# A two-layer graph and feed-forward kernel: the second graph's edge columns packed without rounding each tile to chunks

## The chip, the cores and the metric

The kernel runs on one core of a Trainium2 chip. The metric is device time in microseconds (us) of one execution; the median of three is given, and one further execution was profiled. A core has TensorE (PE in the profile; PEld are its weight loads), VectorE (DVE), ScalarE (ACT), GpSimd (POOL) and SyncE (SP). SP computes nothing: here it starts DMAs and passes on semaphores.

## The reference

Four layers work in turn on x (6250 nodes by 256), each one adding its result to x; each takes the layer norm of x.

```python
# first graph: attention over incoming edges, with encoded edge attributes
alpha = (h_src . a_src) + (h_dst . a_dst) + sum(relu(edge_attr @ edge_W.T + edge_b) * h_dst)
# feed-forward 1: 64 slice tokens for each of 8 heads, attention among the tokens, back to the nodes
# second graph: 106250 edges, 8 heads, no edge attributes
s_u = x @ W_u.T + b_u
s_v = x @ W_v.T
e = leaky_relu(s_u[src] + s_v[dst], 0.2)
probs = exp(e - segment_max(e, dst)[dst]) / segment_sum(exp(...), dst)[dst]
out = segment_sum(x[src] * probs, dst)
# feed-forward 2: 8 experts, the best two for each node
```

Both graphs have the same edges, sorted by their destination. A node's degree is its number of incoming edges, 17 on average.

## The kernel before

**Nodes in tiles.** `sort_nodes` sorts the nodes by degree and puts them into 49 tiles of 128 nodes, one node to a partition. A tile has as many edge columns as its largest degree; column j of a partition holds the j-th edge of its node, or a stand-in for none (source N, a row of zeros whose score is a very low number). For the inputs of the reference the largest degrees of the 49 tiles, counted from `dst`, run from 9 to 35: 9, 10, 11, three of 12, three of 13, four of 14, four of 15, five of 16, five of 17, five of 18, four of 19, three of 20, three of 21, two of 22, two of 23, 25, 26 and 35. They sum to 851.

**Columns in chunks.** C = 4 columns are a chunk. Each tile is rounded up to whole chunks, at least three: 232 chunks or 928 columns in all. `windows` writes them to the array `slots` in DRAM, 64 bytes (4 records of 4 words) for a partition and chunk. `K["ct"]` and `K["lt"]` hold the first and the last chunk of each tile.

**A graph stage** (`graph`, called for layer 0 and layer 1) works through the chunks in order, with R = 4 buffers:

- SP (`load`, L863) brings a chunk's records into `recs`, and (`relay`, L868) passes on that a chunk's rows have landed.
- POOL (`gather`, L900) starts four indirect DMAs per chunk, one for each column; each fetches for 128 partitions the row of the source node. Before it refills a buffer it waits for `msg_ok` of the chunk four places earlier.
- DVE (`body`) makes the scores (L1170, L1172), the running maximum over the tile's chunks (L1176), the differences (L1177); ACT takes the exponentials (L1055); DVE multiplies the rows by them (`messages`, L1133) and rescales the sums that are in PSUM (`rescale`, L1139).
- PE (`aggregate`, L945) adds the chunk's messages to those sums with the identity as weights: four matmuls of 264 columns in fp32, shown as eight.

`by_tile` runs these bodies: the first chunk of a tile (it opens it), a hardware loop (`Fori`) over those between, the last one (it closes it). In the body that opens a tile, DVE also finishes the tile before (`finish`, L1143 to L1157 and L135), after ACT has copied its sums out of PSUM (L1022).

**Between the graphs** stands `slice_ffn`. It is a row of blocks, each with one program for an engine, and at a block's end all engines wait for one another. The block at L1286 (the tokens' sums) has programs for PE, ACT and DVE; SP has none in it and waits at its end. The next blocks, L1447 and L1551, work on the tokens and write the rows of the second graph.

A loop of SP that the prediction uses stands in `windows`, L767 to L773: for each tile one `value_load` of a number into a register, one DMA to an address computed from it, then a wait until that DMA has landed.

Of the kernel before, what the change touches and what calls it, by code (L numbers as in the profile page):

```python
# [11 lines left out]
F32 = mybir.dt.float32  # L12
# [8 lines left out]
E = 106250  # L21
# [27 lines left out]
LEAST = -(-2 * N // Q) // 2 * 2  # L49
KC = HID // 128  # L50
# [30 lines left out]
def take(eng, sem):  # L81

    eng.wait_ge(sem, 1)
    eng.sem_inc(sem, -1)  # L84
# [78 lines left out]
def sort_nodes(nc, K, ins, dr):  # L163


    with ExitStack() as stack:
# [58 lines left out]
        deep = m.sb("o_deep", [1, QT])  # L225
        aim = m.sb("o_aim", [1, QT])
        reach = m.sb("o_reach", [1, QT])
# [30 lines left out]
        with nc.Block() as block:  # L258
# [83 lines left out]
            def _(dve):  # L342
# [90 lines left out]
                ch.link(v.reduce_max(dmax[:], pD[0:QT, :], axis=AX))  # L433
                ch.link(v.tensor_scalar(ci[:], dmax[:], float(C - 1), None, ALU.add))
# [18 lines left out]
                ch.link(v.tensor_scalar(reach[:], pC[:, 2, 0:QT], -3.0, None, ALU.add))  # L453
                v.scalar_tensor_tensor(K["pl"][:], pC[:, 0, 0:QT], 8.0, reach[:], ALU.mult, ALU.add)
                ch.link(v.tensor_scalar(deep[:], pC[:, 2, 0:QT], float(WIN - 1), None, ALU.is_ge))
                ch.link(v.scalar_tensor_tensor(aim[:], pC[:, 0, 0:QT], 3.0, spare[:], ALU.add, ALU.subtract))
                ch.link(v.tensor_tensor(aim[:], aim[:], deep[:], ALU.mult))
                v.tensor_tensor(K["dc"][:], aim[:], spare[:], ALU.add)
# [126 lines left out]

FIRST = 33
# [8 lines left out]
def windows(nc, K, ins, dr, m, dall, ew, recT, ew_in, own_in):  # L595
# [33 lines left out]
    pB = m.ps("x_pB", [Q, 512])  # L629
    w_in = T("w_in"); bxb_ok = T("bxb_ok"); w_ok = T("w_ok"); wch = T("wch")  # L630
# [32 lines left out]
    with nc.Block() as block:  # L663
# [19 lines left out]
        def _(pe):  # L683
            t_ = nc.tensor
            pe.wait_ge(bxb_ok, 1)
# [8 lines left out]
        def _(dve):  # L694
# [4 lines left out]
            v.memset(ew[:], 0.0).then_inc(ew_zero, 1)  # L699
            v.memset(recT[:], 1.0)  # L700
# [3 lines left out]
            wx.link(v.reciprocal(temp, temp))  # L704
            dve.wait_ge(w_ok, 1)
# [77 lines left out]
def graph(nc, K, ins, dr, layer):  # L783
# [7 lines left out]
    with ExitStack() as stack:  # L791
# [27 lines left out]
        else:  # L819
            sdst, norm, wr, raw = K["sdst"], K["norm1"], K["wr"], K["raw"]  # L820
            fin = m.sb(L + "fin", [Q, D])
            turned = m.sb(L + "turned", [128, 2, Q])
# [10 lines left out]
        row_of = lambda ap: ap.rearrange("p a h -> p (a h)")  # L833

# [22 lines left out]
        with nc.Block() as block:  # L857
            @block.sync
            def _(sp):
                n2 = groups(sp, K)  # L860

                def load(u, r):
                    sp.dma_start(recs[:, r, :], dr["slots"][:, bass.ds(4 * u + r, 1), :].rearrange("q a c -> q (a c)").bitcast(F32)).then_inc(rec_in[r], 16)  # L863
# [25 lines left out]
            def _(pool):  # L889
                n2 = groups(pool, K)  # L890
# [22 lines left out]
            def _(pe):  # L913
                t_ = nc.tensor
                n2 = groups(pe, K)
# [21 lines left out]
                def aggregate(i, b):  # L937

                    pe.wait_ge(msg_ok, i + 1)
                    pe.sem_inc(pace, 1)  # L940
# [32 lines left out]
                def body(t, i, opens, closes, ends):  # L973
# [3 lines left out]
                    aggregate(i, bass.ds(i % 2, 1))  # L977
# [125 lines left out]
            def _(dve):  # L1103
# [3 lines left out]
                dve.wait_ge(w_zero, 2)  # L1107
                heads = lambda ap: ap.rearrange("p (c h) -> p c h", h=H)
# [16 lines left out]
                def messages(i):  # L1125

                    b2, b4 = bass.ds(i % 2, 1), bass.ds(i % R, 1)
# [32 lines left out]
                def body(t, i, opens, closes, ends):  # L1160
# [18 lines left out]
                    if first_layer:  # L1179
# [6 lines left out]
                        messages(i)  # L1186
# [4 lines left out]
                    messages(i)  # L1191
# [1012 lines left out]
```

## Time and profile before

| what | us |
|---|---|
| median of 3 executions | 4076.98 (4074.56 to 4084.47) |
| the profiled execution, its own time | 4077.23 |
| its span, first to last instruction | 4075.5 |
| gathers of the second graph, first and last start | 1998.7 and 3159.7 |
| SP's wait at the end of the block at L1286 | 219.6 |

The span is the stretch that the profile's records cover; the execution's own time is 1.7 us more. Stages can be told apart by the tile names: `g_rows<-own` are gathers of the first graph, `g_rows<-rows` those of the second, `f_` the first feed-forward, `e_` the experts.

### The profile page before, as it was taken

Reading aid. Unit: us, or ns where it says so; the run is one execution under the profiler, and the core shown is the slowest. Engines: PE = TensorE matmul, PEld = TensorE weight load, DVE = VectorE, ACT = ScalarE, POOL = GpSimd, SP = SyncE. Lnnn points to the kernel's source line nnn. Section 1 sums busy time; section 2 is a strip of 40 time slices with the busy share of each in tenths; the row PEclk is TensorE's granted clock in tenths of the full one; section 3 lists DMA queues with packets and bytes.
Section 4 is the critical chain, followed back from the end, with each engine's and each line's share of the span. In section 5 each row is a group of like instructions: output and inputs, shape, how many; then the busy total and the mean of one; then the engine's idle time right before and its main releaser. Section 6 shows DMA issues by size and latency. Waiting matters only on the chain. (4 is left out here: it accounts for less than half of the span.)

```text
span 4075.5 us, 69197 instructions
## 1 busy us (share of the span) xinstructions
PE 2987.4 (73%) x12787; PEld 2165.0 (53%) x12788; DVE 2290.8 (56%) x5023; ACT 1295.0 (32%) x5485; POOL 2294.7 (56%) x2343
## 2 busy tenths in 40 slices
PE   4624777788888877989666656566665489999998
PEld 3422444444444444658544444444444388888887
DVE  4534888888888887864355555555555611111111
ACT  1402444444444444432211111111111533333333
POOL 5156777677777772002577777777777523333332
PEclk9857999899999998988777877877777799999999
DMA  8545444344444442000244444444444766665564
GB/s 185 152 92 131 114 115 113 100 106 105 105 105 105 108 108 53 0 2 32 78 112 113 113 113 113 113 112 113 113 113 112 216 186 168 166 170 165 170 174 123
DMA packets 284454, 477.32 MB, mean 117 GB/s; under 512 B 143854, under 2 KB 185660, under 8 KB 283892
## 3 DMA queue, kind: packets, MB, share of 16 engines
q0 software_dynamic: 127312, 321.61, 32.2%
q1 hardware_dynamic: 148203, 151.72, 12.7%
q10 hardware_dynamic: 8880, 3.34, 0.4%
q8 instruction: 21, 0.34, 0.0%
q14 instruction: 38, 0.31, 0.0%
HBM read 426.29 MB, written 50.68 MB: 117 GB/s over the span
## 5 line engine op out<-in xcount | busy, mean ns | idle before, releaser
L945 PE MATMUL g_pA<-g_msg,k_ident 128*128 128x264 f32 (+1 forms) x3712 | 1153.1, 464 | 475.5 <-DVE g_pA L1139 411.6
L945 PEld LDWEIGHTS g_pA<-g_msg,k_ident 128*128 128x128 f32 x3712 | 808.4, 229 | 808.7 <-issue 661.9
L900 POOL DMA_INDIRECT g_rows<-own,g_recs x928 | 879.4, 948 | 333.9 <-issue 262.8
L900 POOL DMA_INDIRECT g_rows<-rows,g_recs x928 | 879.6, 948 | 296.6 <-issue 194.7
L934 PE MATMUL g_pE<-g_ew,g_recT 128*128 128x512 f32 x932 | 515.4, 680 | 242.1 <-DVEq L1123 238.8
L1133 DVE TENSOR_TENSOR g_msg<-g_rows,g_pp 128x1024 f32 (+3 forms) x464 | 571.9, 1233 | 151.4 <-DVEq L84 151.3
L1983 POOL DMA_INDIRECT out<-e_ys,e_goal x102 | 160.6, 1575 | 505.8 <-issue 486.3
L934 PEld LDWEIGHTS g_pE<-g_ew,g_recT 128*128 128x128 f32 x932 | 171.4, 203 | 459.1 <-DVEq L1123 331.2
L2036 PE MATMUL e_pY<-e_w,e_hT 128*128 x1632 | 373.8, 382 | 35.5 <-issue 35.5
L1055 ACT ACTIVATE g_pp<-g_dd 128x32 f32<-128x32 f32 x464 | 95.2, 205 | 918.5 <-ACTq L84 918.5
L2025 PEld LDWEIGHTS e_pH<-e_xT,e_w 128*128 128x128 f32 x3264 | 381.6, 192 | 5.2
L2025 PE MATMUL e_pH<-e_xT,e_w 128*128 128x128 f32 x3264 | 381.9, 275 | 0.0
L2122 DVE TENSOR_TENSOR e_ys<-e_pY,k_x 128x256 f32<-128x256 f32 x102 | 43.3, 425 | 581.8 <-PE e_pY L2036 575.4
L2036 PEld LDWEIGHTS e_pY<-e_w,e_hT 128*128 128x128 f32 x1632 | 302.0, 190 | 84.1 <-issue 47.1
L1166 DVE TENSOR_REDUCE g_al<-g_prod 128x32 f32<-128x1088 f32 x232 | 297.1, 1280 | 57.7 <-DVEq L84 57.7
L1118 DVE SCALAR_TENSOR_TENSOR g_prod<-g_pE,g_dall 128x1024 f32<-128x1024 f32 x232 | 284.2, 1225 | 20.6 <-DVEq L84 7.8
L1069 ACT ACTIVATE g_pA<-g_pA,g_cs 128x33 f32<-128x33 f32 x1464 | 276.3, 277 | 4.4
L1006 ACT ACTIVATE g_recT<-g_pRT 16x128 f32<-16x128 f32 x234 | 62.2, 266 | 541.4 <-ACTq L84 541.0
L2078 ACT ACTIVATE e_hT<-e_pH,e_b 128x128 f32<-128x128 f32 x816 | 221.7, 382 | 39.3 <-issue 36.5
L2065 ACT ACTIVATE e_xT<-e_pX,e_bl,e_gl 128x128 f32<-128x128 f32 x204 | 82.2, 453 | 462.0 <-PE e_pX L2008 462.0
L1170 DVE TENSOR_TENSOR g_al<-g_rows,k_sdst 128x32 f32 (+1 forms) x232 | 45.0, 194 | 287.0 <-DVEq L84 282.3
L1561 POOL MEMSET f_bu<- 128x16 f32 x1 | 0.1, 111 | 288.7 <-POOLq L113 288.7
(419 smaller groups left out, 3533.5 us busy)
## 6 DMA issues: line engine op xcount, KB each, us to landing
e_w<-in_L_ffn_W SPq DMA_DIRECT2D x110, 1024.0 KB
g_rows<-own,g_recs POOLq DMA_INDIRECT x928
g_rows<-rows,g_recs POOLq DMA_INDIRECT x928
g_recs<-slots SPq DMA_DIRECT2D x468, 8.0 KB
tok<-e_xall SPq DMA_DIRECT2D x7, 910.0 KB
own<-p_row SPq DMA_DIRECT2D x50, 119.0 KB
p_x<-in_x SPq DMA_DIRECT2D x1, 5600.0 KB
own<-p_x SPq DMA_DIRECT2D x1, 5600.0 KB
```

What stands on the lines that cost most here:

```text
L900: pool.indirect_dma_start(out=rows[:, r, j, :], out_offset=None, in_=rows_d, in_offset=bass.IndirectOffsetOnAxis(ap=recs[:, r, 4 * j:4 * j ...
L934: last = t_.matmul(pE[:, c:c + 512], recT[:], ew[:].rearrange("p c d -> p (c d)")[:, c:c + 512], start=True, stop=True)
L945: last = t_.matmul(sums, K["ident"][:], of, start=False, stop=(j == C - 1), skip_group_check=True)
L1055: s.activation(pp[:, 0:C * H], dd[:, 0:C * H], ACT.Exp).then_inc(pp_ok, 1)
L1069: last = s.activation(of[:, h, :], of[:, h, :], ACT.Copy, scale=cs[:, h:h + 1])
L1118: v.scalar_tensor_tensor(to, pE[:].rearrange("p (c h w) -> p c h w", c=C, h=H), 0.0, over(by_head(own), 1, C), ALU.max, ALU.mult).then_inc ...
L1133: v.tensor_tensor(to, of, by, ALU.mult).then_inc(msg_ok, 1)
L1166: ch.link(v.reduce_sum(sc, prod[:], axis=AX))
L1983: pool.indirect_dma_start(out=out, out_offset=bass.IndirectOffsetOnAxis(ap=goal_b[b][:, 0:1], axis=0), in_=ys[:, b, :], in_offset=None, bo ...
L2025: last = t_.matmul(pH[b][c][:, j, :], w1[:, b, k, units], xT[:, b, k, :], start=(k == 0), stop=(k == 1))
L2036: last = t_.matmul(pY[b][:], hT[:, b, k, :], w2[:, bass.ds(e, 1), k, :].rearrange("p a h -> p (a h)"), start=(k == 0), stop=(k == KC - 1))
L2078: last = s.activation(hT[:, b, c * HK + j, :], pH[b][c][:, j, :], ACT.Gelu, bias=b1[:, bass.ds(e, 1), c * HK + j])
```

## The change

The second graph no longer reads `slots` but a new array `cols`, in which the tiles' columns follow one another with no rounding. A tile has max(largest degree, 8) columns, so there are 851, in 213 chunks; gathers go by groups of four chunks, so 54 groups or 216 chunks are fetched. `K["at"]` holds the first column of each tile, `K["ends_in"]` the chunk in which the tile before it ends. A chunk in which one tile ends and the next begins is fetched once and worked on twice: by the body that closes the one (columns past its end are masked with `past`) and by the body that opens the other (columns ahead of its start are masked with `ahead`). This is done at all 48 borders, also where a tile ends with a chunk; there are 213 + 48 = 261 bodies in place of 232. The buffer of a shared chunk comes free with the second of them, and POOL now waits for the semaphore `freed`, which PE raises in `aggregate`.

`cols` is filled by a new program for SP in the block at L1286 of the kernel before: for each tile it copies the tile's chunks from `slots` to `cols`, DRAM to DRAM, to the tile's first column, and waits until all of them have landed, since the next tile's copy overwrites what the last chunk has beyond its columns.

Smaller edits: `sort_nodes` and `windows` compute the new tables; `past` and `ahead` are made by five DVE instructions at the second graph's start; the memset of `oz` stands later in its block; some buffers share memory.

```diff
@@ windows: DVE
+            dve.wait_ge(pF_ok, 1)
+            v.tensor_copy(K["at"][:], pF[:, 0:QT + 1])
+            wx.link(v.tensor_scalar(K["ends_in"][:], pF[:, 0:QT + 1], -1.0, None, ALU.add))
+            wx.link(v.tensor_scalar(K["ends_in"][:], K["ends_in"][:], CLOG, None, ALU.arith_shift_right))
@@ graph
+        at = (lambda t, i: i) if first_layer else (lambda t, i: i + t)
         def bounds(eng, t):
+            if not first_layer:
+                last_of = lambda x: eng.value_load(K["ends_in"][0:1, bass.ds(x, 1)], min_val=1, max_val=COLS // C)
+                return 0 if isinstance(t, int) and t == 0 else last_of(t), last_of(t + 1)
@@ graph: POOL
-                            pool.wait_ge(msg_ok, 4 * (u - 1) + (r + 1))
+                            pool.wait_ge(done, 4 * (u - 1) + (r + 1))
@@ graph: PE
                     pe.wait_ge(msg_ok, i + 1)
-                    pe.sem_inc(pace, 1)
+                    pe.sem_inc(freed if frees else pace, 1)
...
-                    aggregate(i, bass.ds(i % 2, 1))
+                    aggregate(i + t, bass.ds((i + t) % 2, 1), not closes)
@@ graph: DVE, before the first body
+                    mc.link(v.scalar_tensor_tensor(inside[:], K["ends_in"][:], -float(C), K["at"][:], ALU.mult, ALU.add))
+                    mc.link(v.tensor_tensor(past[:], over(K["iota64"][:, 0:C], 1, QT), over(inside[:, 1:QT + 1], 2, C), ALU.is_ge))
...
@@ graph: DVE, body
-                        take(dve, rows_ok)
+                        if start or not opens:
+                            take(dve, rows_ok)
...
+                    if not first_layer and (closes or opens and not start):
+                        of = (past if closes else ahead)[:, bass.ds(t, 1), :]
+                        ch.link(v.tensor_tensor(heads(sc), heads(sc), over(row_of(of), 2, H), ALU.add))
@@ slice_ffn: a program for SP in the block of the tokens' sums
+                    def piece(chunk, col, n, put):
+                        sp.dma_start(dr["cols"][:, bass.ds(col, C * n), :].rearrange("q a c -> q (a c)"),
+                                     dr["slots"][:, bass.ds(chunk, n), :].rearrange("q a c -> q (a c)")).then_inc(put, 16)
+                    with sp.Fori(0, QT) as t:
+                        chunk = sp.value_load(K["ct"][0:1, bass.ds(t, 1)], min_val=0, max_val=CMAX - 2 * WIN)
+                        close = sp.value_load(K["lt"][0:1, bass.ds(t, 1)], min_val=2, max_val=CMAX - WIN)
+                        col = sp.value_load(K["at"][0:1, bass.ds(t, 1)], min_val=0, max_val=COLS)
+                        with sp.Fori(chunk, close + 1) as i:
+                            piece(i, nc.s_assert_within(col + C * i - C * chunk, 0, COLS), 1, packed)
+                        sp.wait_ge(packed, 16 * close + 16)
+                        sp.sem_inc(pace, 1)
```

What stood in SP's row between the loads of the first feed-forward's weights (L1250) and the load of the next block (L1450), before:

```order
L1250 DMA f_wqkv<-in_L0_ffn_W_q 64x64
L1250 DMA f_wqkv<-in_L0_ffn_W_k 64x64
L1250 DMA f_wqkv<-in_L0_ffn_W_v 64x64
L1243 UNCONDITIONAL_BRANCH
L1448 UNCONDITIONAL_BRANCH
L1450 DMA f_bout<-in_L0_ffn_b_out 128x256
```

And of the change, in the same place, from the third of three such loads of a table into a register (`k_ct` and `k_lt` are loaded just above it) to the end of the loop over tiles (L1334); the loop over a tile's chunks is L1338:

```order
L1337 TENSOR_LOAD k_at
L1337 ISA x2
L1338 UNCONDITIONAL_BRANCH
L1338 ISA
L1339 REGISTER_ALU
L1339 ISA
L1332 ISA
L1332 DMA cols<-slots 128x16
L1338 ISA
L1338 COMPARE_AND_BRANCH
L1340 ISA
L1334 REGISTER_ALU
```

SP has gained a loop with a wait inside (L1340 sets up the wait for the landing), run 49 times, in a block in which it did nothing.

On DVE, the body that closes a tile of the second graph, before:

```order
L1170 ISA
L1170 TENSOR_TENSOR g1_al<-g1_rows,k_sdst 128x32
L1172 SCALAR_TENSOR_TENSOR g1_al<-g1_al 128x32
L1176 TENSOR_REDUCE g1_mx<-g1_al 128x8
L1177 TENSOR_TENSOR g1_dd<-g1_al,g1_mx 128x40
L1133 ISA
L1133 TENSOR_TENSOR g1_msg<-g1_rows,g1_pp 128x1056
L1139 TENSOR_TENSOR g1_pA<-g1_pA,g1_cs 128x8x33
```

And of the change:

```order
L1207 ISA
L1207 TENSOR_TENSOR g1_al<-g1_rows,k_sdst 128x32
L1211 TENSOR_TENSOR g1_al<-g1_al,g1_past 128x32
L1212 SCALAR_TENSOR_TENSOR g1_al<-g1_al 128x32
L1216 TENSOR_REDUCE g1_mx<-g1_al 128x8
L1217 TENSOR_TENSOR g1_dd<-g1_al,g1_mx 128x40
L1169 ISA
L1169 TENSOR_TENSOR g1_msg<-g1_rows,g1_pp 128x1056
L1175 TENSOR_TENSOR g1_pA<-g1_pA,g1_cs 128x8x33
```

One small instruction has come in (L1211); the body that opens a tile has gained its like with `g1_ahead`. The bodies between are as they were.

## Rows read from the trace of the kernel before

**Rows 1.** The page: span, and busy time by engine (share of the span)

```profile
span 4075.5 us, 69197 instructions
PE 2987.4 (73%) x12787; PEld 2165.0 (53%) x12788; DVE 2290.8 (56%) x5023; ACT 1295.0 (32%) x5485; POOL 2294.7 (56%) x2343
```

**Rows 2.** Windows: the tokens' block, then the second graph

```profile
core 0: us, PE busy (x) PEld busy (x) DVE busy (x) ACT busy (x) POOL busy (x), PEclk, DMA share, GB/s
1590.00:1809.00 219.00, 211.06 (x882) 139.09 (x882) 175.84 (x298) 93.75 (x197) 0.00 (x0) 0.98 0.00 1
1998.00:3164.00 1166.00, 703.57 (x2125) 506.34 (x2126) 621.63 (x1577) 161.60 (x885) 879.59 (x928) 0.78 0.45 113
```

**Rows 3.** Line L900 in the second graph: durations ns, first and last start

```profile
L900 POOL DMA_INDIRECT g_rows<-rows,g_recs x928: 942/946/1189, 1998.7 to 3159.7; - x186
  issue: 194.7, 639
```

**Rows 4.** Timeline of DVE: a closing body, an opening one, a middle one

```profile
2512.97 0.19 DVE L1170 TENSOR_TENSOR g_al<-g_rows,k_sdst 128x32 f32 x1 [3.40 <-DVEq L84]
2513.19 0.19 DVE L1172 SCALAR_TENSOR_TENSOR g_al<-g_al 128x32 f32<-128x32 f32 x1
...
2517.03 0.19 DVE L1170 TENSOR_TENSOR g_al<-g_rows,k_sdst 128x32 f32 x1 [0.91 <-DVEq L84]
...
2518.56 1.25 DVE L1133 TENSOR_TENSOR g_msg<-g_rows,g_pp 128x1056 f32 x1 [0.64 <-DVEq L84]
2521.02 0.17 DVE L1143 TENSOR_SCALAR g_den<-g_accf 128x8 f32<-128x8 f32 x1 [1.20 <-DVEq L84]
...
2523.38 0.20 DVE L1170 TENSOR_TENSOR g_al<-g_rows,k_sdst 128x32 f32 x1
...
2526.48 0.19 DVE L1170 TENSOR_TENSOR g_al<-g_rows,k_sdst 128x32 f32 x1
```

**Rows 5.** Timeline of PE in the same stretch

```profile
2516.47 3.88 PE L945 MATMUL g_pA<-g_msg,k_ident 128*128 x8 [4.29 <-DVE g_pA L1139]
...
2526.88 2.04 PE L945 MATMUL g_pA<-g_msg,k_ident 128*128 x8 [1.59 <-DVE g_pA L1139]
```

**Rows 6.** Timeline of all engines: middle bodies that follow at once

```profile
3098.39 0.18 DVE L1170 TENSOR_TENSOR g_al<-g_rows,k_sdst 128x32 f32 x1
...
3098.82 3.56 PE L945 MATMUL g_pA<-g_msg,k_ident 128*128 x8 [3.53 <-DVE g_pA L1139]
...
3102.78 0.44 DVE L1139 TENSOR_TENSOR g_pA<-g_pA,g_cs 128x264 f32<-128x264 f32 x1 [1.59 <-DVEq L84]
...
3103.53 0.19 DVE L1170 TENSOR_TENSOR g_al<-g_rows,k_sdst 128x32 f32 x1 [0.30 <-DVEq L84]
```

**Rows 7.** Timeline of DVE: last middle body of tile 5, its closing body

```profile
2087.31 0.19 DVE L1170 TENSOR_TENSOR g_al<-g_rows,k_sdst 128x32 f32 x1
...
2090.95 0.19 DVE L1170 TENSOR_TENSOR g_al<-g_rows,k_sdst 128x32 f32 x1 [0.49 <-DVEq L84]
```

**Rows 8.** Timeline: a chunk's fourth gather, and its scores

```profile
2528.36 0.95 POOL L900 DMA_INDIRECT g_rows<-rows,g_recs  x1 [0.30 <-issue]
...
2531.48 0.19 DVE L1170 TENSOR_TENSOR g_al<-g_rows,k_sdst 128x32 f32 x1 [1.71 <-DVEq L84]
```

**Rows 9.** Waits of SP: total us, times, longest

```profile
SPq L1286 <- PEq L1286: 219.6, 1, 219.6
```

**Rows 10.** Timeline of SP: start, then first issue to end of last

```profile
100.28 25.89 SPq L280 DMA_DIRECT2D own<-p_row  x38
...
317.54 9.94 SPq L771 DMA_DIRECT2D slots<-x_win  x3
```

**Rows 11.** Line L771, SP's loop with a wait: last its landing times

```profile
L771 SPq DMA_DIRECT2D slots<-x_win x3: 342/343/348, 317.5 to 327.1; - x3
...
DMA to landing us min/median/max: 3.0/3.3/3.4
```

**Rows 12.** Line L770, the register load of that loop

```profile
L770 SPq FUSED_REGOPS  x6: 37/102/164, 316.6 to 326.6; - x6
L770 SPq TENSOR_LOAD <-k_dc x3: 273/275/275, 316.7 to 326.3; - x3
L770 SPq SEQ_ASSERT  x3: 18/18/18, 317.2 to 326.8; - x3
```

**Rows 13.** DMA issues: KB each, median us to landing

```profile
slots<-x_more SPq DMA_DIRECT2D x1, 64.0 KB, 1.6
```

More of the change, by code:

```diff
@@ L684, in _ @@
             t_ = nc.tensor
+            pe.wait_ge(wide_ok, 1)
+            t_.matmul(pF[:, 0:QT + 1], colw[:], K["tri"][0:QT, 0:QT + 1], start=True, stop=True).then_inc(pF_ok, 1)
             pe.wait_ge(bxb_ok, 1)
@@ L821, in graph @@
             fin = m.sb(L + "fin", [Q, D])
+            inside = m.sb(L + "inside", [Q, QT + 1])
+            past = m.sb(L + "past", [Q, QT, C])
+            ahead = m.sb(L + "ahead", [Q, QT, C])
+            masks = m.sem(L + "masks")
             turned = m.sb(L + "turned", [128, 2, Q])
@@ L859, in _ @@
             def _(sp):
-                n2 = groups(sp, K)
+                n2 = groups(sp, K) if first_layer else column_groups(nc, sp, K)
                 def load(u, r):
-                    sp.dma_start(recs[:, r, :], dr["slots"][:, bass.ds(4 * u + r, 1), :].rearrange("q a c -> q (a c)").bitcast(F32)).then_inc(rec_in[r], 16)
+                    of = dr["slots"][:, bass.ds(4 * u + r, 1), :] if first_layer else dr["cols"][:, bass.ds(4 * C * u + C * r, C), :]
+                    sp.dma_start(recs[:, r, :], of.rearrange("q a c -> q (a c)").bitcast(F32)).then_inc(rec_in[r], 16)
                 def relay(u, r):
@@ L889, in _ @@
             def _(pool):
-                n2 = groups(pool, K)
+                n2 = groups(pool, K) if first_layer else column_groups(nc, pool, K)
+                done = msg_ok if first_layer else freed
                 def gather(u, first):
@@ L914, in _ @@
                 t_ = nc.tensor
-                n2 = groups(pe, K)
+                n2 = groups(pe, K) if first_layer else None
                 def transpose(u, r):
@@ L1107, in _ @@
                 dve.wait_ge(w_zero, 2)
+                if not first_layer:
+                    mc = Chain(dve, masks)
+                    mc.link(v.scalar_tensor_tensor(inside[:], K["ends_in"][:], -float(C), K["at"][:], ALU.mult, ALU.add))
+                    mc.link(v.tensor_tensor(past[:], over(K["iota64"][:, 0:C], 1, QT), over(inside[:, 1:QT + 1], 2, C), ALU.is_ge))
+                    mc.link(v.tensor_tensor(ahead[:], over(K["iota64"][:, 0:C], 1, QT), over(inside[:, 0:QT], 2, C), ALU.is_lt))
+                    mc.link(v.tensor_scalar(past[:], past[:], -LOW, None, ALU.mult))
+                    mc.link(v.tensor_scalar(ahead[:], ahead[:], -LOW, None, ALU.mult))
                 heads = lambda ap: ap.rearrange("p (c h) -> p c h", h=H)
@@ L1185, in body @@
                         take(dve, pp_ok)
-                        messages(i)
+                        messages(t, i)
                         if not ends:
@@ L1190, in body @@
                     take(dve, pp_ok)
-                    messages(i)
+                    messages(t, i)
                     if opens:
@@ L1285, in slice_ffn, with _ @@
             g3 = lambda ap: ap.rearrange("p (h g) -> p h g", h=FH)
+            packed = T("packed"); last_packed = T("last_packed")
             with nc.Block() as block:
+                @block.sync
+                def _(sp):
+                    def piece(chunk, col, n, put):
[9 more added lines that the diff above has]
+                        sp.sem_inc(pace, 1)
+                    piece(sp.value_load(K["end"][:], min_val=0, max_val=CMAX - WIN), sp.value_load(K["at"][0:1, QT:QT + 1], min_val=0, max_val=COLS), 4, last_packed)
+                    sp.wait_ge(last_packed, 16)
                 @block.tensor
@@ L1520, in _ @@
                     v.tensor_tensor(g3(at[:]), g3(pq[:]), over(red[:], 2, G), ALU.subtract).then_inc(exp_in, 1)
+                    v.memset(oz, 0.0)
                     dve.wait_ge(exp_out, 1)
@@ L1698, in experts @@
             hot = [m2.sb(f"e0_hot{k}", [Q, QT, X]) for k in range(2)]
-            both = m2.sb("e0_both", [Q, QT, X])
+            both = K["sdst"]
             best = [m2.sb(f"e0_best{k}", [Q, QT]) for k in range(2)]
@@ L2162, in program @@
               "slots": scratch("slots", (Q, CMAX + 3 * QT, REC), I32),
+              "cols": scratch("cols", (Q, COLS + 16 * C, C), I32),
               "tok": scratch("tok", (1 + NPAD, XW))}
```

47 lines of the change are left out of this document (28 added, 19 removed).

## The prediction

> **What bounds the kernel now.** I read the page first, for the span [rows 1]. No engine is busy throughout, so the stages must be told apart. Two matter here, and the windows show them [rows 2]. In the block of the tokens' sums PE is busy for 211 of 219 us, and the DMA share is 0.00: PE bounds it, and SP and the DMA engines do nothing. In the second graph no engine reaches 80% busy, yet POOL is the bound. That takes the line's own view: 928 gathers start between 1998.7 and 3159.7, one each 1161/927 = 1.252 us, of which 0.946 us is the instruction and 0.3 us is put down to issue (194.7 us in 639 times) [rows 3]. The reader is to see that POOL never stands still: a chunk of four gathers takes 5.0 us, 232 chunks take 1161 us, and that is the stage.
>
> Next, how near the others are. The timeline of DVE gives the time from one body to the next where nothing holds it up. From the body that closes a tile to the first middle body of the next it is 2523.38 - 2512.97 = 10.4 us, with the opening body between; from a middle body to the next it is 3.10 us [rows 4]. The first of these was with PE at 1.2 GHz (eight matmuls in 3.88 us); at 2.4 GHz they take 2.04 us [rows 5]. Where PE is at 1.2 GHz a middle body takes 5.14 us, since the rescaling must wait for the sums of the body before [rows 6]. From the last middle body to the closing one I read 3.64 us [rows 7]. The granted clock over the stage is 0.78 of full speed [rows 2], so both kinds occur.
>
> **The second graph after the change.** POOL starts 864 gathers in place of 928: 64 x 1.252 = 80 us less. It gets this only if the bodies keep up, and there are 29 more of them. A tile with k bodies costs DVE: closing to first middle 10.4 us, less at most 1.2 us with PE at 2.4 GHz (the opening body's messages end at 2519.81, so `finish` cannot start much sooner than that, where it started at 2521.02 [rows 4]), plus two masks. A mask is one instruction of 128x32 like L1172, at 0.19 us and a gap: 0.22 us. I take 10.3 us. Last middle to closing costs 3.7 us, and each further middle body lies between 3.10 and 5.14 us; I take 3.5 us, nearer the lower end, because PE has less idle time when bodies follow at once. So a tile costs 14.0 + 3.5 (k - 3) us, against 1.252 us of POOL for each column.
>
> The first 22 tiles (largest degree 9 to 16) have 301 columns and, counting the borders, 97 bodies. DVE needs 22 x 14.0 + 31 x 3.5 = 416.5 us, POOL 377 us: DVE falls 40 us behind. From there the two go about level (a tile of 17 columns and 5 bodies: 21.0 against 21.3 us), and only the last tiles give time back. The four buffers take up part of the lag: a chunk's scores can start 3.1 us after its fourth gather [rows 8], that is 6.9 us after its first; its buffer is wanted 20 us after its first, 13 us later, and a body holds it for 3 us: about 10 us. POOL is then held up by some 32 us, and the stage gets 80 - 32 = 48 us shorter. The bounds: with every body at 2.4 GHz (13.3 + 3.1 (k - 3)) the lag is about 12 us, nearly all taken up, and the gain is 78 us. With middle bodies at 4.0 us the lag reaches some 80 us by the same sum and the gain is about 10 us; with all at 5.1 us the stage would be longer than now, which I leave out of the range, since PE would then hardly be idle and its clock would rise.
>
> The hand-over of a buffer through PE (`freed`) costs POOL nothing where PE waits for the messages anyway. What DVE does before its first body, the five mask instructions of at most 128x196, lies beside the first gathers, which have to land first.
>
> **The copy.** Here the change adds a chain of its own, in a block that is 219.6 us long for SP [rows 9]. SP waited there for the others; now it has 49 tiles with 232 DMAs, and the others will wait for it.
>
> Per DMA: 38 DMAs with one computed address were issued in 25.89 us, 0.68 us each, some waiting included [rows 10]. The new one has a second address and sits in a loop with a branch at each turn; I add 0.27 us (four short register instructions with their gaps, of the kind of 37 to 102 ns each [rows 12]): 0.95 us, 232 x 0.95 = 220 us. Bounds 0.85 and 1.05 us.
>
> Per tile: three register loads. One is 0.275 + 0.16 + 0.02 us with gaps [rows 12], 0.65 us with its address; three are 1.95 us. Then the wait for landing. The nearest loop in the trace, one load, one DMA, one wait, takes (9.94 - 0.34)/2 = 4.8 us a turn [rows 10], of which 3.3 us is landing [rows 11]. That leaves 1.5 us for load, address and branch, which bears out these prices. How long a 64-byte piece takes from DRAM to DRAM no row shows. The rows around it are 1.6 us for the 64 KB of `x_more` [rows 13] and 3.3 us for the 24 KB pieces of `x_win`, which were issued beside POOL's gathers. In the new place nothing else uses the DMA engines, so I take 2.0 us, of which 0.7 us lies under the DMA's own issue and the inner branch: 1.3 us. Control of both loops and the semaphores: 0.85 us. Together 4.1 us, 49 x 4.1 = 201 us. With the last piece of four chunks and its wait (4 us) the copy takes 220 + 201 + 4 = 425 us and starts with the block. It sticks out of it by 425 - 219.6 = 205 us. Nothing hides that: the next block's first work waits at the barrier. Bounds: 0.85 us and 1.6 us to landing give 197 + 181 + 4 = 382 us, 162 us over; 1.05 us and 3.3 us give 244 + 265 + 4 = 513 us, 293 us over.
>
> The Trainium skill, in "DMA: Bandwidth & Descriptors", gives a fixed cost of about 2.0 us for a DMA (Anatomy of one DMA), and lists 512 B as the least transfer without a read-modify-write (Specifications). The first would leave my sum as it is. The second speaks for a later landing of 64-byte pieces; it is a rival below, priced from rows.
>
> **The rest.** The memset of `oz` moves from the head of its block to a place beside ACT's exponentials; both are under 1 us, and I count nothing. The tables in `sort_nodes` and `windows` are four or five instructions of under 0.3 us beside gathers.
>
> **Sum.** Against the profiled execution's 4077.2 us, which stands level with the median of 4077.0: + 205 - 48 = + 157, so 4234 us.
>
> **Rivals.**
> 1. *Late landing.* Pieces smaller than those of `x_win` land no sooner than these did, 3.3 us, though no gathers run. Then each tile waits 1.3 us longer: 64 us, 4298 us. For it: of the two rows, the one with the smaller pieces has the longer time. Against it: those ran beside other traffic.
> 2. *The bodies eat the gain.* PE stays at 1.2 GHz for most of the stage, middle bodies take 4 us and more, and the second graph saves 10 us or nothing: 4272 to 4282 us. For it: a clock of 0.78 now. Against it: PE's idle time before L945 shrinks when bodies follow at once.
> 3. *The copy is hidden*, and the kernel is faster. SP would have to be through in 219.6 + 48 = 268 us to break even, 5.5 us a tile with its 4.7 DMAs. Were the DMAs 0.5 us each and three loads and the wait 2.9 us, it would be 262 us, and the time 4071; fully hidden it would be 4029. Against it: the loop of L771 needs 4.8 us a turn for one load and one DMA [rows 10, 11]. It decides as soon as a chunk costs less than 0.5 us in all.
> 4. *The packing does nothing for the gathers*: POOL is still held up at each border, and only the copy is left. This is rival 2 at its end.
>
> **How the numbers follow.** The forecast, copy 380 to 460 us and a gain of 20 to 78 us, has 60%: its own range is 4165 to 4290. Rival 1 has 20%, rival 2 12%, rival 3 6%; 2% for anything else. 80% lie between 4170 and 4310: the lower end is the quick copy with nearly the full gain, the upper the late landing and little gain. 0.3% is 12 us, about what can be told from no change. Faster by more than that only in rival 3: 6%. Within it 1%. Slower 93%.
>
> **What would show it.** In the block of the tokens' sums the engines' busy time stays as in [rows 2], but the block is some 425 us long, and PE waits for SP at its end. The DMAs from `slots` to `cols` stand 0.9 to 1.0 us apart within a tile and 4 to 5 us across one. The gathers are 864, and between first and last start some 1113 us; if they take 1082, DVE never held POOL up. The mean time of L945's matmuls tells rival 2 from the forecast. I am wrong if SP's loop is through before PE is, or if the landing is not waited for once a tile.

## The result, and the profile after

The changed kernel takes 4444.73 us (median of 4 runs, 4435.65 to 4456.38) against 4075.77 us before (again the median of 4): ratio 1.0903, 95% interval 1.0871 to 1.0936. It is slower, as predicted, but by 369 us and not by 157; the forecast of 4234 us and its range up to 4310 both miss. The profiled execution took 4440.49 us. From here "before" is the kernel before and "after" the changed one.

The page of after, its first two lines (they answer to [rows 1]):

```profile
span 4438.7 us, 73650 instructions
PE 2993.2 (67%) x13021; PEld 2166.9 (49%) x13022; DVE 2373.9 (53%) x5304; ACT 1305.0 (29%) x5572; POOL 2236.6 (50%) x2279
```

No engine has more to do than before by more than DVE's 83 us, while the span grew by 363: the loss is waiting. Two windows, the tokens' block and the second graph, say where (they answer to [rows 2]):

```profile
core 0: us, PE busy (x) PEld busy (x) DVE busy (x) ACT busy (x) POOL busy (x), PEclk, DMA share, GB/s
1576.00:2168.00 592.00, 211.33 (x882) 139.51 (x882) 175.90 (x299) 93.91 (x197) 0.00 (x0) 0.68 0.04 4
2354.00:3545.00 1191.00, 732.69 (x2382) 518.84 (x2382) 707.23 (x1861) 174.39 (x981) 819.52 (x864) 0.80 0.40 102
```

In the first, PE is busy for the same 211 us as in [rows 2], but the block lasts 592 us in place of 219. In the second, POOL has 64 gathers and 60 us of work less, and the stage is longer all the same. The gathers' own line, first in the first graph, then in the second with what POOL waited for (to [rows 3]):

```profile
L929 POOL DMA_INDIRECT g_rows<-own,g_recs x928: 940/946/1181, 342.9 to 1550.6; - x186
...
L929 POOL DMA_INDIRECT g_rows<-rows,g_recs x864: 940/946/1192, 2355.0 to 3539.2; - x173
its engine sat idle before it (us, times) until:
  issue: 249.2, 762
  PEq L969: 113.3, 91
```

The same line of before, in its first graph:

```profile
L900 POOL DMA_INDIRECT g_rows<-own,g_recs x928: 940/946/1181, 344.3 to 1564.0; - x186
```

These starts cut both spans into stages, of which the last is what follows the last gather (to 4438.7 and 4075.5):

| stage | before, us | after, us | difference |
|---|---|---|---|
| up to the first gather | 344.3 | 342.9 | -1.4 |
| first graph | 1219.7 | 1207.7 | -12.0 |
| between the graphs, with the copy | 434.7 | 804.4 | +369.7 |
| second graph | 1161.0 | 1184.2 | +23.2 |
| behind the last gather | 915.8 | 899.5 | -16.3 |

I had +205 for the third row, -48 for the fourth and nothing for the others.

**The copy.** The line of the DMA (durations in ns, first and last start), and the register operations of the inner loop's own line, two in a turn:

```profile
L1332 SPq DMA_DIRECT2D cols<-slots x233: 547/564/687, 1579.2 to 2165.7; - x117
DMA to landing us min/median/max: 2.0/2.1/3.4
...
L1338 SPq FUSED_REGOPS  x464: 42/156/273, 1578.5 to 2162.7; - x155
```

The waits (us in all, times, longest): SP's for the landing at a tile's end, and PE's behind its own part of the block, before its first matmul of the next.

```profile
SPq L1341 <- DMA cols<-slots: 58.6, 49, 2.2
...
PE f_pA L1516 <- DVE f_sums L1562: 375.9, 1, 375.9
```

SP is at work from 1576 to 2168 us without a pause but for 58.6 us. Its timeline, two DMAs of one tile:

```profile
1597.53 2.40 SPq L1332 DMA_DIRECT2D cols<-slots  x2
```

From the start of the first to the end of the second it is 2.40 us; less one DMA of 0.57, they stand 1.83 us apart. Over all neighbours within a tile the mean is 1.79 us, where I had 0.95.

**The second graph.** DVE's timeline, which answers to [rows 4]. L1207 is the first instruction of a body. The rows are those of one tile from its first middle body on (three middle ones from 2702.02, the closing one at 2712.05), the opening and the first middle body of the next, and then two middle bodies of a later tile; the other instructions and bodies are left out:

```profile
2702.02 0.19 DVE L1207 TENSOR_TENSOR g_al<-g_rows,k_sdst 128x32 f32 x1 [0.20 <-issue]
...
2705.24 0.18 DVE L1207 TENSOR_TENSOR g_al<-g_rows,k_sdst 128x32 f32 x1
...
2708.83 0.19 DVE L1207 TENSOR_TENSOR g_al<-g_rows,k_sdst 128x32 f32 x1 [0.29 <-issue]
...
2712.05 0.18 DVE L1207 TENSOR_TENSOR g_al<-g_rows,k_sdst 128x32 f32 x1
...
2717.01 0.19 DVE L1207 TENSOR_TENSOR g_al<-g_rows,k_sdst 128x32 f32 x1 [1.35 <-issue]
...
2722.86 0.19 DVE L1207 TENSOR_TENSOR g_al<-g_rows,k_sdst 128x32 f32 x1 [0.20 <-issue]
...
2748.82 0.18 DVE L1207 TENSOR_TENSOR g_al<-g_rows,k_sdst 128x32 f32 x1
...
2754.24 0.19 DVE L1207 TENSOR_TENSOR g_al<-g_rows,k_sdst 128x32 f32 x1 [0.40 <-DVEq L86]
```

and PE's in the same stretches (to [rows 5, 6]):

```profile
2705.68 2.04 PE L974 MATMUL g_pA<-g_msg,k_ident 128*128 x8 [1.81 <-DVE g_pA L1175]
...
2712.52 2.04 PE L974 MATMUL g_pA<-g_msg,k_ident 128*128 x8 [1.59 <-DVE g_pA L1175]
...
2749.26 3.88 PE L974 MATMUL g_pA<-g_msg,k_ident 128*128 x8 [2.57 <-DVE g_pA L1175]
...
2754.18 3.88 PE L974 MATMUL g_pA<-g_msg,k_ident 128*128 x8 [1.04 <-DVE g_pA L1175]
```

From a middle body to the next there are three prices. The first pair of a tile takes 3.22 us (2702.02 to 2705.24), since the rescaling finds the opening body's sums ready. A later pair takes 3.59 us with PE at 2.4 GHz (2705.24 to 2708.83; the matmuls between them last 2.04 us), and 5.42 us with PE at 1.2 GHz (2748.82 to 2754.24; 3.88 us), since the rescaling waits for the sums of the body before. Closing to opening is 4.96 us here, opening to middle 5.85. Taking the starts of this line one after another over tiles 0 to 38, where DVE from tile 1 on lags behind the gathers by 7 to 21 us and so nothing but the bodies sets the pace, gives the means below.

| from one body to the next, tiles 0 to 38 | times | predicted, us | after, us | more in all, us |
|---|---|---|---|---|
| closing to opening to middle | 38 | 10.3 | 5.09 + 5.73 | 20 |
| last middle to closing | 39 | 3.7 | 3.82 | 5 |
| middle to middle | 74 | 3.5 | 4.09 (32 of them over 4) | 44 |

In tiles 0 to 38 the 74 pairs of middle bodies fall apart by those prices: 37 are the first of their tile (3.21 to 3.22 us), 5 are later ones at 3.59 us, and 32 are later ones of 4.29 to 5.43 us, 5.18 on the mean, with PE at 1.2 GHz for at least part of the matmuls that are waited for. The 69 us are nearly all of the 71 by which this stage missed its term. The gathers' starts show the same from POOL's side: summed over the chunks, they are 105 us later than one chunk each 5.0 us, where I had 32, and nearly all of it before 3240 us.

### The profile page after: what moved, and what is told of

It reads as the page before. It is cut to its first block and busy times, and to the rows that moved or that the text cites. A ratio compares the mean times of both kernels' runs of the same rounds, so it can differ in the third digit from the quotient of the medians.

```text
span 4438.7 us, 73650 instructions
## 1 busy us (share of the span) xinstructions
PE 2993.2 (67%) x13021; PEld 2166.9 (49%) x13022; DVE 2373.9 (53%) x5304; ACT 1305.0 (29%) x5572; POOL 2236.6 (50%) x2279
## 5 line engine op out<-in xcount | busy, mean ns | idle before, releaser
L974 PE MATMUL g_pA<-g_msg,k_ident 128*128 (+1 forms) x3944 | 1173.5, 449 | 464.2 <-DVE g_pA L1175 336.0
L974 PEld LDWEIGHTS g_pA<-g_msg,k_ident 128*128 128x128 f32 x3944 | 822.8, 219 | 811.4 <-issue 672.4
L929 POOL DMA_INDIRECT g_rows<-rows,g_recs x864 | 819.5, 949 | 378.9 <-issue 249.2
L1169 DVE TENSOR_TENSOR g_msg<-g_rows,g_pp 128x1056 f32 (+3 forms) x493 | 608.2, 1234 | 209.4 <-DVEq L86 209.4
```

The costliest lines, as they stand in the source:

```text
L929: pool.indirect_dma_start(out=rows[:, r, j, :], out_offset=None, in_=rows_d, in_offset=bass.IndirectOffsetOnAxis(ap=recs[:, r, 4 * j:4 * j ...
L974: last = t_.matmul(sums, K["ident"][:], of, start=False, stop=(j == C - 1), skip_group_check=True)
L1169: v.tensor_tensor(to, of, by, ALU.mult).then_inc(msg_ok, 1)
```

## Experiments

All are compared with runs of before on the same chip as theirs (medians 4078.2, 4083.0, 4079.7 and 4080.1 us in the four sets).

**1. The copy alone.** All of the copy, none of the packed reading:

```diff
-n2 = groups(pool, K) if first_layer else column_groups(nc, pool, K)
+n2 = groups(pool, K)
...
-of = dr["slots"][...] if first_layer else dr["cols"][...]
+of = dr["slots"][:, bass.ds(4 * u + r, 1), :]
...
-if not first_layer and (closes or opens and not start):
+if False:
```

> The columns are copied as in the change, but the second graph then reads the slots as before: 232 bodies, no masks, no packed columns (the copied columns are not used). Theory A (the copy block costs what the trace of the changed kernel shows: 592 us where the block took 219.6): 4075.8 + 372 = 4448, less up to 13 us by which the first graph came out shorter there, so 4435 to 4450. Theory B (the copy costs the 205 us of my prediction and the rest of the loss lies in the second graph): about 4281.

Measured: 4421.27 us, ratio 1.0840 (1.0822 to 1.0858). Theory B is out: the copy by itself loses 343 us. The time lies 14 us under A's interval, of which some 9 are that the rest of the change gives back 22 us (experiment 9) and not 13.

**2. Packed reading, and columns that cost nothing.** Eight straight copies in the place of the loop. They leave the columns where they were, so this kernel sums other edges, as many as before, in the 261 bodies of the change (the expectation below has 265 by mistake):

```diff
-with sp.Fori(0, QT) as t:
-    ...
+for k in range(8):
+    sp.dma_start(dr["cols"][:, 108 * k:108 * (k + 1), :]..., dr["slots"][:, 27 * k:27 * (k + 1), :]...)
```

> The second graph is the changed one (packed columns, 265 bodies, masks), but the columns come from 8 straight copies of 27 chunks each and no loop over tiles: arranging the columns is left out, so the sums of the second graph are of other edges, as many as before. Theory A (216 gathered chunks in 265 bodies are no faster than 232, since bodies and not GpSimd bound the first 39 tiles: 1184 us of gathers against 1161): 4075.8 + 23, less up to 13 us of the first graph, so 4080 to 4105. Theory B (the second graph by itself gains the 48 us that I predicted and its loss is an effect of the copy ahead of it): 4015 to 4030.

Measured: 4071.44 us, ratio 0.9978 (0.9949 to 1.0008), ten runs between 4028 and 4087. The second graph took 1187.5 us from first to last gather, as in after (A), and the copy's 370 us are gone. The median lies 9 us under A's interval. The 22 us of experiment 9 in place of 13 would make up for that; by before's 4078.2, the second graph's 26.5 and these 22 it should still be 4083, so 12 us are not explained. The eight DMAs, with fixed addresses and 1728 B a partition, take 0.597 us of SP each:

```profile
L1332 SPq DMA_DIRECT2D cols<-slots x8: 592/597/604, 1577.0 to 1581.5; - x8
```

**3. No wait at a tile's end.** Each chunk goes to its own place, and one wait stands behind both loops. This too leaves out the arranging of the columns:

```diff
-piece(i, nc.s_assert_within(col + C * i - C * chunk, 0, COLS), 1, packed)
-sp.wait_ge(packed, 16 * close + 16)
+piece(i, nc.s_assert_within(C * i, 0, COLS), 1, packed)
...
+sp.wait_ge(packed, 16 * last + 16)
```

> Every chunk is copied to its own place (4 columns a chunk), so that no copy overlaps another and the wait for the landing at each tile's end goes; one wait stands behind the loop. Arranging the columns is left out. Theory A (SP's turns of 1.79 us for each of 232 copies are the cost, and the 49 landing waits, 58.6 us, come on top): 4445 - 56 = 4389, 4378 to 4395; the SP loop takes 535 us instead of 592. Theory B (the transfers themselves are what SP waits for, and its issue slows down because the queue is full): no change, 4440 to 4450. Theory C (the wait also holds the pace of the loop, so that without it the turns get as short as the 0.95 us that I predicted): 4190 to 4210.

Measured: 4316.28 us (four runs, 4300 to 4335), ratio 1.0600 (1.0572 to 1.0628): 128 us less than after, and none of the three theories' numbers. The line of its DMA, and the inner loop's register operations:

```profile
L1332 SPq DMA_DIRECT2D cols<-slots x233: 522/543/682, 1583.0 to 2033.2; - x117
DMA to landing us min/median/max: 1.9/2.0/3.3
...
L1338 SPq FUSED_REGOPS  x464: 42/59/87, 1582.6 to 2030.4; - x155
```

and two DMAs of one tile in its timeline:

```profile
1707.66 1.99 SPq L1332 DMA_DIRECT2D cols<-slots  x2
```

The DMAs now stand 1.99 - 0.53 = 1.46 us apart (1.48 as the mean), since with the wait I also took out the arithmetic on the column (`col + C * i - C * chunk`). Of the two operations of L1338 in a turn one takes 0.04 us in both kernels; the other takes 0.26 us in after and 0.07 here, and an addition on L1339 is gone as well. 0.31 us less for 232 DMAs is 71 us, and the 58.6 us of waits make 130. So nobody waits for the queue (B is out), and the turns come nowhere near 0.95 us (C is out): SP's own instructions are the cost. Beside the DMA's 0.54 to 0.57 us the loop takes 0.93 us a turn here and 1.22 in after.

**4. Matmuls that keep TensorE busy.**

```diff
 last.then_inc(agg_ok, 1)
+if not first_layer:
+    for _ in range(4):
+        t_.matmul(pX[:, 0:128], K["ident"][:], K["ident"][:], start=True, stop=True)
```

> The changed kernel with four matmuls of 128 columns behind the four of each body of the second graph, into a PSUM bank that nothing reads, in the time in which TensorE waits for VectorE's rescaling. Theory A (middle bodies take 4.9 to 5.4 us instead of 3.2 to 3.6 because TensorE runs at 1.2 GHz in them, and a busier TensorE is granted 2.4 GHz more of the time): the second graph comes near GpSimd's bound of 216 x 5.0 = 1082 us, so 30 to 90 us less than the changed kernel: 4355 to 4415, with a granted clock near 1 in the second graph. Theory B (the granted clock does not follow TensorE's work here): the clock stays near 0.80 and the time at 4445 or, where the added 0.9 to 1.8 us a body lie on the chain, up to 4600.

Measured: 4376.80 us, ratio 1.0735 (1.0717 to 1.0753): 68 us less than after, by work that nobody needs. The window of its second graph (the last but two of the numbers is the clock):

```profile
2351.00:3481.00 1130.00, 859.57 (x4470) 728.94 (x4470) 702.48 (x1860) 178.07 (x981) 819.72 (x864) 0.93 0.42 108
```

The granted clock rose from 0.80 to 0.93, POOL's wait for buffers (`PEq L970`) fell to 55.3 us, and the gathers took 1125.2 us. In tiles 0 to 38 middle bodies came down from 4.09 to 3.56 us, last middle to closing from 3.82 to 3.35; opening bodies stayed at 5.77, which hang on DVE. Only 11 of the 74 middle pairs were still over 4 us. Theory A holds, though not in full: the clock is 0.93 and not 1, and the stage is still 43 us above POOL's 1082.

**5. One copy a tile.**

```diff
-with sp.Fori(0, QT) as t:
-    ...
+piece(0, 0, 9, packed)
+with sp.Fori(1, QT) as t:
+    chunk = ...; col = ...
+    sp.wait_ge(packed, 16 * t)
+    sp.sem_inc(pace, 1)
+    piece(chunk, col, 9, packed)
```

> The changed kernel, its columns copied in 50 DMAs instead of 233: one of 9 chunks (36 columns, 576 B a partition) for each tile, since no tile here has over 35 columns; what it writes behind its tile's columns the next tile's copy overwrites, and each still waits for the one before to land. The two registers of a tile are loaded before that wait. Nothing is left out. Theory A (the loop's cost is SP's turns for single chunks): a landing of 2.1 to 3.4 us and some 0.6 us of issue for each of 49 tiles, 130 to 200 us, less than the 219.6 us for which the block's other engines work; then the time is that of the straight copies, 4055 to 4085. Theory B (copies of DRAM to DRAM are slow by their bytes, so that nine times the bytes land much later): with over 4.5 us a tile the block is longer than 219.6 us, and the time over 4090.

Measured: 4068.84 us, ratio 0.9956 (0.9933 to 0.9979), twelve runs from 4038 to 4087. The whole loop now stands in the block's shadow. Its DMA line:

```profile
L1332 SPq DMA_DIRECT2D cols<-slots x50: 557/567/609, 1576.3 to 1712.9; - x50
```

SP's wait at the end of the block, then the windows of the block and of the second graph:

```profile
SPq L1327 <- PEq L1327: 80.5, 1, 80.5
```

```profile
1576.00:1795.00 219.00, 211.08 (x882) 139.23 (x882) 175.18 (x297) 93.82 (x197) 0.00 (x0) 0.98 0.08 18
...
1982.00:3161.00 1179.00, 727.07 (x2382) 516.81 (x2382) 705.98 (x1860) 174.35 (x980) 818.94 (x864) 0.81 0.40 103
```

A tile takes (1712.9 - 1576.3)/49 = 2.8 us, and nine times the bytes cost nothing in issue: 0.567 us as against 0.564. The block is at its 219 us again, and SP waits 80.5 us for the others instead of they for it. The runs' times go with their granted clock: 4038 us at 0.890, 4087 at 0.872, the others between. That fits a stage which hangs on PE; before's 23 runs spread over 11 us only.

**6. Both.** The edits of experiments 4 and 5 together.

> One copy a tile and the four matmuls behind each body of the second graph together. Theory A: the gains add, so 4376.8 (with matmuls alone) less the copy's 366 us: 4000 to 4020, the first version under the kernel before. Theory B (with the copy gone, the second graph starts from another state of the clock and the matmuls bring less): 4020 to 4070.

Measured: 4008.72 us, ratio 0.9822 (0.9808 to 0.9837), 74 us under before. The granted clock of its second graph is 0.93, as in experiment 4. The line of its gathers, which take 1120.9 us:

```profile
L930 POOL DMA_INDIRECT g_rows<-rows,g_recs x864: 942/949/1202, 1983.5 to 3104.4; - x173
its engine sat idle before it (us, times) until:
  issue: 242.4, 760
  PEq L970: 54.1, 89
```

**7. The same matmuls in the kernel before.**

> The kernel before with the same four matmuls behind each body of its second graph. Theory A (its second graph goes by GpSimd's gathers at 5.00 us a chunk throughout, so TensorE's clock costs nothing there): 4070 to 4082, as without them. Theory B (the matmuls help there as well, so that packing the columns has no part in what they bring): 4000 to 4060.

Measured: 4080.59 us, ratio 0.9997 (0.9988 to 1.0006). The clock rose there too:

```profile
1995.00:3164.00 1169.00, 832.28 (x3965) 700.24 (x3966) 618.87 (x1577) 164.61 (x885) 881.79 (x928) 0.87 0.45 112
```

but POOL's gathers take 1163.4 us as ever. A faster PE is worth something only once the bodies are the bound, and packing is what made them so.

**8. No masks.** A chunk that two tiles share then counts in full in both.

```diff
-if not first_layer and (closes or opens and not start):
+if False:
```

> The changed kernel without the 97 additions of masks in closing and opening bodies (the mask tables are still made), which leaves out that a chunk shared by two tiles counts only its own columns in each. Theory A (in the first 39 tiles the chain over the bodies sets the time, and a closing and an opening body each lose 0.22 us on it): 77 x 0.22 = 17 us less, 4420 to 4432. Theory B (the mask additions lie beside TensorE's matmuls): within 5 us of the changed kernel.

Measured: 4418.39 us, ratio 1.0829 (1.0814 to 1.0845), 26 us less than after (34 if each is taken against its own before); the gathers took 1155.8 us instead of 1184.2. From an opening body to the next it is 5.26 us instead of 5.73; from a closing one 5.09 as in after. So the opening mask is on the chain (39 x 0.47 = 18 us), with 0.3 us of its own and some of the address arithmetic around it, and the closing one is not. Middle bodies, which have no mask, had a mean of 3.90 instead of 4.09 us: 26 in place of 32 were over 4 us, which may be the clock's scatter, and the longest took 5.30 and not 5.43, for which I have no cause.

**9. The rest of the change.** Experiment 1 without SP's loop:

```diff
-@block.sync
-def _(sp):
-    def piece(chunk, col, n, put):
-    ...
```

> The change without its two main parts: no column is copied, and the second graph reads the slots in 232 bodies without masks. What is left is the rest: the column counts, the scratch tiles that now share memory, the moved memset of the attention block, the space for the columns, and with them other places of all code that follows. Theory A (the 12 us by which the first graph, and the 11 to 24 us by which everything behind the last gather came out shorter in all changed kernels, come from this rest): 4078 - 12 - 12 = 4054, 4045 to 4060. Theory B (they come from the copy or the packed reading): 4072 to 4084, as before.

Measured: 4058.04 us, ratio 0.9944 (0.9930 to 0.9957): 21.6 us under before. The first graph's gathers:

```profile
L929 POOL DMA_INDIRECT g_rows<-own,g_recs x928: 940/946/1183, 345.3 to 1554.5; - x186
```

1209.2 us, as in every changed kernel (1208 to 1209), where before has 1219.7. Theory A as to the time. Of what the last stage gained in after (16.3 us) the trace here has 6.5, so that part is not wholly the rest's.

**10. The opening mask added beforehand.**

```diff
+for c in range(C):
+    mc.link(v.tensor_tensor(opening[:, :, c * H:(c + 1) * H], sdst[:], over(ahead[:, :, c:c + 1]..., 2, H), ALU.add))
-if not first_layer and (closes or opens and not start):
+if not first_layer and closes:
```

> One copy a tile, the four matmuls, and the mask of the opening bodies added beforehand to the table of target scores (one table of 32 numbers a tile, four additions in all), so that an opening body has no mask addition of its own; the closing body keeps its own. Theory A (without masks an opening body took 5.26 us to the next instead of 5.73 in the first 39 tiles, and nothing else changed there; so the opening mask alone is on the chain): 39 x 0.47 = 18 us less than 4008.7, where bodies set the pace: 3985 to 4000. Theory B (with TensorE at 2.4 GHz most of that time is GpSimd's, only 41 us of its gathers are late, and they start elsewhere): within 5 us of 4008.7.

Measured: 4002.81 us, ratio 0.9819 (0.9806 to 0.9833), against 0.9822 without the table: 76.9 us under its own before, where it was 74.3. Theory B, by these differences (the bare times lie 5.9 us apart, just over its 5): opening bodies got shorter (5.51 instead of 5.77 us), middle ones longer (3.61 for 3.52), and the 39 tiles took 800 us as against 801. With PE at 2.4 GHz most of their pace is POOL's: 39 tiles have 612 columns, 766 us of gathers at 1.252 us each.

**11. Shared scratch tiles alone.** The kernel before with `deep`, `aim`, `reach`, `oz` and `both` placed as in the change.

> The kernel before with one piece of the change's rest: the scratch tiles that share memory with others (three of the degree sort, one of the attention block with its memset moved, one of the router). Theory A (shared places of tiles are what makes the first graph 11 us and what is behind the last gather 6 us shorter in the rest alone): 4079.7 - 21.6 = 4058, 4053 to 4063. Theory B (the cause is elsewhere in the rest: the places of instructions, or of the buffers in HBM behind the new column buffer): 4073 to 4084, as before.

Measured: 4078.90 us, ratio 0.9997 (0.9988 to 1.0006). Theory A is out.

**12. Two matmuls.** As experiment 6, with `range(2)`.

> One copy a tile, and two matmuls of 128 columns behind each body of the second graph instead of four (4068.8 us with none, 4008.7 with four). Theory A (what they bring comes through TensorE's granted clock in the second graph, which lies between 0.80 without and 0.94 with four there): a clock between, and a time in proportion, 4025 to 4055. Theory B (any work in those gaps does it, whatever its length): a clock and a time as with four, 4003 to 4015.

Measured: 4004.30 us, ratio 0.9821 (0.9807 to 0.9836), as with four, at a clock of 0.90 in the second graph (0.93 with four). Theory B, so far as the time goes; from 0.90 to 0.93 the clock buys nothing more here.

## Why the prediction was right in its direction and wrong in its size

**What bounds the kernel now: right.** PE bounds the tokens' block and POOL the second graph. Experiment 7 is the check: a higher clock changes nothing in the kernel before.

**Where the 211 us come from.** The time is 4445 us and the forecast was 4234. By the stages of the two traces, where it makes 206 us, the copy cost 165 us more than its term, the second graph 71 more, and the rest, counted at nothing, gave 30 back. Two terms of the sum failed: the DMA at 0.95 us and the middle body at 3.5 us. (The forecast's own range, 4165 to 4290 us, comes to 4160 to 4298 by its terms, which changes nothing.)

**The copy, per DMA: this step failed.** I took 0.95 us, bounds 0.85 and 1.05; it was 1.79 us. 232 x 0.84 = 195 us, of which a tile's end and start, taken too long, hid 29. Two things were in it. The 0.68 us came from DMAs of [rows 10] that keep SP for 0.32 us each (0.34 in [rows 11]); this one takes 0.564. With 576 B a partition it is 0.567, and with fixed addresses and 1728 B 0.597 (experiment 2), so neither the bytes nor the second computed address make it; what is left that these have in common is that both ends are in DRAM, which no experiment varied. And the loop's instructions took 1.22 us where I had 0.34 + 0.27 beside the DMA: four register operations on counter, chunk and column, a check of their range, two moves and a branch, with their gaps. Experiment 3 prices the arithmetic on the column alone at 0.31 us. I had counted "four short register instructions" from a loop that computes one address, though the diff shows two, one of them with three operands. Writing out the sequence would not have been enough: in the trace of before no register operation of SP is longer than 0.19 us, where the one for the column takes 0.26, and none of its DMAs goes from DRAM to DRAM.

**The copy, per tile: right in its parts.** Landing 2.1 us (2.0 taken; rival 1 had 3.3, and is refuted). The waits for it come to 58.6 us, 1.2 a tile (1.3 taken). All of the tile's end and start makes (592 - 232 x 1.79 - 4)/49 = 3.5 us; 4.1 was taken. Each of the three loads is 0.65 us with its gaps, as said. The Trainium skill, in "DMA: Bandwidth & Descriptors" (Anatomy of one DMA), gives a fixed cost of about 2.0 us for a DMA issued from GpSimd; the 2.1 us of SP's DMAs here agree with it. The same page has 512 B as the least size without a read-modify-write (Specifications). In the time to landing nothing of it shows: 64-byte pieces took 2.1 us.

**Nothing hides it: right.** 592 - 219.6 = 372 us over the block, and 369.7 between the last gather of one graph and the first of the next. Rival 3 named the point from which the copy would be hidden (268 us for SP); experiment 5 is on its other side with 139 us, and indeed not slower.

**The second graph: the mechanism right, the size wrong, and its sign with it.** That 29 more bodies make DVE fall behind in the tiles of few columns, that the lag goes through the four buffers to POOL, and that only the last tiles give time back, all came so. The term that failed is the middle body at 3.5 us: it was 4.09, because PE was at 1.2 GHz for 32 of the 74 pairs. I chose near the lower end "because PE has less idle time when bodies follow at once". The granted clock rose from 0.78 to 0.80 only. The loop from the sums of one body over DVE's rescaling to the next sums leaves PE idle for over 1 us even when nothing is late (2754.18: 1.04 us). The lower end was also misread: the 3.10 us of [rows 4] are the first middle body behind an opening one, whose rescaling waits for nothing. A later one took 3.59 us at best here, and 5.42 at 1.2 GHz. That was rival 2, to which I gave 12%, and its end at "no gain" fell short still: the stage took 23 us more. I had left out a longer stage since "its clock would rise", which is the same unfounded step again. Experiment 4 shows that the clock was the matter: in experiments 4 and 6, with it at 0.93, the 39 tiles took 807 and 801 us against 869, and my sum for them by 3.5 us was 800.

The Trainium skill says in "TensorE: Matmul & The Clock Gate" (Part 1) that activity releases the throttle. The trace agrees in direction: with more matmuls in the same gaps the granted clock rose from 0.80 to 0.93.

The second part of this miss is closing to opening, 5.09 us instead of the 4.06 of [rows 4] and a mask. It is not the mask: without masks it was 5.09 as well (experiment 8). The closing body's rescaling waits for the sums of the last middle body, and the loads of the next tile's bounds stand behind that wait (part of the 1.35 us put down to issue at 2717.01). In 37 of the 38 the opening body starts 2.45 to 2.48 us after those sums end (here from 2712.52 + 2.04 = 2714.56 to 2717.01), with masks and without. [rows 4] was read where PE had long been done.

**The rest, which I counted at nothing: wrong by 22 us.** Experiment 9 shows them as a gain. It was luck: like the tile's term it hid part of the two misses above. Without them the change would cost 391 us. Experiment 11 takes the shared tiles and the moved memset out as a cause; open are the few added table instructions and the places of the instructions and of the buffers in HBM that lie behind the new one. None was tried alone, so the cause stays open.

**The account.** The rest -21.6 (experiment 9), the copy +364.7 (experiment 1's +343.1 less that), and the packed reading +25.9 (after's +369.0 less experiment 1's), each against its own before. The stages of the trace, taken from single executions, say nearly the same: +369.7 between the graphs, +23.2 in the second graph, -29.7 in the other three.

## What to carry to other kernels

Price a loop of small DMAs by writing out every instruction of one turn on the engine that issues them, both addresses, checks and branch included, and multiply by the turns; then ask whether one larger DMA a tile, overlapping the next, does the same (232 turns of 1.79 us became 49 of 2.8, from 592 us to 139). When a change takes work off the bounding engine, work out what the loop behind it costs at both clocks of PE, and from a row in which the loop's own waits stand; where the trace before has the low clock in such a stage (0.78 here), more work in the same loop is no reason to price it at the high one. Where such a loop is the bound, a few matmuls on a spare PSUM bank in that wait can be worth more than the change itself (68 us in after), and where it isn't they are worth nothing.

## What the runs showed that I had not expected

- In SP's queue a DMA from DRAM to DRAM takes 0.564 us with 64 B a partition and 0.567 with 576 B, where one from `x_win` took 0.34 [rows 11]. With fixed addresses and 1728 B it is 0.597.
- In all eleven kernels that hold the rest of the change, which has no instruction of note in these stages, the first graph was 10 to 12 us shorter, and what follows the last gather 6 to 24 us; in the two that don't (experiments 7 and 11) these stages stayed as before or grew a little.
- The packed kernels' runs spread over 48 us with one copy a tile (twelve runs, 4038 to 4087, clock 0.890 to 0.872) and over 12 us with four matmuls a body (four runs, 4001 to 4012): the matmuls seem to steady the time as well.
